# Two-layer gated cross-attention with experts: where layer 1's attention takes its statistics and moments

## The reference, cut to what matters

```python
x = x + jnp.tanh(g_xattn[0]) * _L0_xattn_ref(_layernorm(x), ctx, ctx, ...)   # 16 heads
x = x + jnp.tanh(g_ffn[0])   * _L0_ffn_ref(_layernorm(x), ...)               # 8 experts, each token takes its best 2
x = x + jnp.tanh(g_xattn[1]) * _L1_xattn_ref(_layernorm(x), ctx, ctx, ...)   # one head, causal mask
x = x + jnp.tanh(g_ffn[1])   * _L1_ffn_ref(_layernorm(x), ...)               # each expert takes its best 17 tokens of a sequence
```

## Time and profile before

| | us |
|---|---|
| median of 3 runs | 1018.54 |
| lowest and highest of them | 1015.94, 1024.3 |
| the profiled execution's own time | 1020.45 |
| its span, first to last instruction | 1018.6 |
| mean granted clock of TensorE, of full speed | 0.963 |

### The profile page before, as it was taken

One profiled execution on the slowest core, in us unless ns is written; L12 is line 12 of the kernel. 1 busy time (PEld: TensorE's weight loads), 2 busy tenths in 40 slices (PEclk: granted clock), 3 DMA queues, 4 the chain that ended last, 5 costly groups with the idle time before them and its releaser, 6 DMA issues.

```text
span 1018.6 us, 25355 instructions
## 1 busy us (share of the span) xinstructions
PE 901.6 (89%) x9084; PEld 745.5 (73%) x9084; DVE 590.7 (58%) x1580; ACT 550.4 (54%) x1313; POOL 645.3 (63%) x807
## 2 busy tenths in 40 slices
PE   5998999888439999999999989778998999999992
PEld 3776767667328989899999966655776766778881
DVE  5887989999526473245625669774635325433320
ACT  1787877776314545444654766535554555454440
POOL 6453455368753777677427777721886658878885
PEclk9999999999759999999999999898999999999996
DMA  9365333012524656776556663140444634565454
GB/s 369 120 198 170 140 143 129 27 60 72 180 84 138 215 166 209 216 214 191 167 183 194 189 241 105 58 125 31 100 42 48 134 27 53 99 88 55 51 57 44
DMA packets 130156, 130.73 MB, mean 128 GB/s; under 512 B 33010, under 2 KB 102770, under 8 KB 129138
## 3 DMA queue, kind: packets, MB, share of 16 engines
q1 hardware_dynamic: 99810, 91.66, 28.9%
q0 software_dynamic: 28928, 29.91, 17.8%
q10 hardware_dynamic: 1296, 7.54, 1.8%
HBM read 53.84 MB, written 49.62 MB: 102 GB/s over the span
## 4 chain that ended last, share of the span: by engine, by line
PE 60%; DVE 11%; issue 9%; POOL 8%; DMA 7%; ACT 4%; SPq 1%; ACTq 0%; POOLq 0%; DVEq 0%
PE psum L881 11%; PE psum L897 11%; PE psum L1070 8%; PE psum L1060 8%; PE psum L687 3%; PE psum L1024 3%; PE psum L674 2%; DVE w_sb L1211 2%; POOL xg L2072 2%; PE psum L704 2%; POOL work L2086 2%; PE psum L871 2%; POOL odd L2164 1%; DMA odd<-ln_sb,dest 1%; DMA x_sb<-in_x 1%
## 5 line engine op out<-in xcount | busy, mean ns | idle before, releaser
L1858 ACT ACTIVATE hid_sb<-psum,work 128x128 f32<-128x128 f32 (+1 forms) x424 | 145.4, 411 | 157.4 <-PE psum L881 155.4
L2086 POOL DMA_INDIRECT work<-yg,place x128 | 122.8, 959 | 62.6 <-issue 35.1
L881 PE MATMUL psum<-work 128*128 128x128 f32 (+1 forms) x848 | 151.7, 322 | 4.0 <-issue 3.7
L897 PE MATMUL psum<-w_sb,hid_sb 128*128 x1192 | 150.2, 275 | 0.0
L897 PEld LDWEIGHTS psum<-w_sb,hid_sb 128*128 128x128 f32 x1192 | 144.7, 192 | 2.1
L1060 PE MATMUL psum<-work,w_sb 128*128 128x272 f32 (+2 forms) x512 | 131.1, 397 | 5.1 <-ACT ctx_sb L1959 3.1
L881 PEld LDWEIGHTS psum<-work 128*128 128x128 f32 x848 | 125.1, 193 | 13.7 <-issue 6.3
L2164 POOL DMA_INDIRECT out_x<-ln_sb,dest x68 | 106.0, 1559 | 44.9 <-DVE ln_sb L1665 25.0
L2072 POOL DMA_INDIRECT xg<-work,place x104 | 100.5, 966 | 53.4 <-issue 25.6
L1959 ACT ACTIVATE ctx_sb<-psum,w_sb 128x272 f32<-128x272 f32 (+2 forms) x256 | 115.8, 487 | 26.4 <-PE psum L1060 22.6
L1070 PE MATMUL psum<-ctx_sb,w_sb 128*128 128x272 f32 (+2 forms) x512 | 128.1, 392 | 0.0
(11 more groups left out here) (264 smaller groups left out, 1570.0 us busy)
## 6 DMA issues: line engine op xcount, KB each, us to landing
work<-w_sb SPq DMA_DIRECT2D x76, 322.0 KB
work<-xg SPq DMA_DIRECT2D x73, 128.0 KB
yg<-yg_sb SPq DMA_DIRECT2D x73, 128.0 KB
xg<-yg_sb SPq DMA_DIRECT2D x24, 384.0 KB, 4.1
ctx_sb<-tok SPq DMA_DIRECT2D x8, 1088.0 KB, 6.2
ctxn<-sums_sb SPq DMA_DIRECT2D x64, 64.0 KB
out_x<-x_sb SPq DMA_DIRECT2D x16, 256.0 KB, 2.2
odd<-yg_sb SPq DMA_DIRECT2D x10, 384.0 KB, 3.1
```

Of the source, the lines that this page charges most:

```text
L881: e.matmul(banks[UP_BANKS[c]][:, 0:cols], w1g(b)[:, c * P:c * P + P], xgT_sb[:, u % 2, at:at + cols], start=True, stop=True).then_inc(s_up, 1)
L897: ins = e.matmul(banks[DOWN_BANKS[b % 2]][:, n * D:n * D + D], hid0[:, b % 2, c, n * P:n * P + P], w2_sb[:, bass.ds(number, 1), c, :].rear ...
L1858: e.activation(hid0[:, b % 2, c, 0:cols], banks[UP_BANKS[c]][:, 0:cols], ACT.Gelu, bias=w1g(b)[:, HID + c:HID + c + 1]).then_inc(s_hg, 1)
L2086: e.indirect_dma_start(dst[:, k, :], None, yg_dram[h], at).then_inc(s_get[i], 16)
```

## The change

Routing starts two steps earlier, in step 5. The lists leave behind the store of group 9 instead of 11. Six tiles are picked in the loop instead of four, in steps 13 to 15. From step 3 on `LATER_BY` is one tile behind the old one, from step 5 on two. Router statistics of groups 0 to 3 are taken in steps 2 to 5 and those of groups 4 to 7 in steps 12 to 15. GpSimd's order becomes: gathers 48 and 49, `moments1(40)`, gathers 50 to 55, one chain of router moments for all 16 tiles, gathers 56 to 59, `moments1(48)`, gathers 60 to 63, `moments1(56)`, one chain for tiles 16 to 31. A chain over n tiles counts its semaphore by n // 8, so that the waits on it stay as they are.

```diff
--- before.py
+++ after.py
@@ -103,7 +103,7 @@
 
 NORM1_FROM = NBLK[0] + NBLK[1] + 14
 
-ROUTE1_FROM = 7
+ROUTE1_FROM = 5
 
 
 ROUTE_IN = {NP - 1: 1, NP: 2, NP + 1: 1, NP + 2: 1}
@@ -111,10 +111,10 @@
 COUNT_AT, SOFTMAX_AT, GATES_AT = 11, 12, 18
 
 
-SPREAD_AT = 11
-PICKED = {14: (0, 1), 15: (2, 3)}
-
-LATER_BY = (0, 1, 3, 5, 7, 9, 11, 13, 15, 16)
+SPREAD_AT = 9
+PICKED = {13: (0, 1), 14: (2, 3), 15: (4, 5)}
+
+LATER_BY = (0, 1, 3, 4, 6, 7, 9, 11, 13, 15, 16)
 
 
 def later_by(u):
@@ -123,6 +123,7 @@
 
 
 EARLY_ROUTER = 2 * NS // TG
+ROUTER_STATS = {2: 0, 3: 1, 4: 2, 5: 3, 12: 4, 13: 5, 14: 6, 15: 7}
 
 RING = 32
 
@@ -1628,8 +1629,8 @@
                     combine(t)
                     if t % TG == TG - 1:
                         statistics1(t // TG)
-                if 5 <= u < 5 + EARLY_ROUTER:
-                    statistics_router1(u - 5)
+                if u in ROUTER_STATS:
+                    statistics_router1(ROUTER_STATS[u])
                 if u >= ROUTE1_FROM:
                     next(side, None)
                 for t in PICKED.get(u, ()):
@@ -2002,8 +2003,8 @@
                 if raised:
                     step.done(ins)
                     ins = e.tensor_scalar(nmr[:, lo:lo + n], nmr[:, lo:lo + n], 1.0, None, ALU.add)
-                ins.then_inc(s_done, 1)
-                made[s_done.num] += 1
+                ins.then_inc(s_done, n // TS or 1)
+                made[s_done.num] += n // TS or 1
                 w.wait_ge(s_done, made[s_done.num])
 
             def moments_twice(router, first):
@@ -2118,8 +2119,8 @@
             def moments1(lo):
                 moments(lo, TS, s_st2, lo + TS, s_mom1, raised=True)
 
-            def moments_router1(lo):
-                moments(lo, TS, s_st3, lo + TS, s_mom2)
+            def moments_router1(lo, n=TS):
+                moments(lo, n, s_st3, lo + n, s_mom2)
 
 
             for t in range(PARTS[-1][0]):
@@ -2134,12 +2135,12 @@
                 get(t)
                 if t == PARTS[-1][0] + 1:
                     moments1(PARTS[-1][0] - TS)
-            moments1(PARTS[-1][0])
-            for lo in range(0, NS, TS):
-                moments_router1(lo)
+                if t == PARTS[-1][0] + 7:
+                    moments_router1(0, NS)
+                if t == PARTS[-1][0] + 11:
+                    moments1(PARTS[-1][0])
             moments1(NT - TS)
-            for lo in range(NS, 2 * NS, TS):
-                moments_router1(lo)
+            moments_router1(NS, NS)
```

## The result

| | before | after |
|---|---|---|
| median, us | 1018.66 (4 runs) | 1027.26 (4 runs) |
| lowest and highest | 1015.94, 1024.3 | 1025.33, 1029.66 |
| ratio, 95% interval | | 1.0083 (1.0049 to 1.0117) |
| profiled execution, its span | 1020.45, 1018.6 | 1025.33, 1023.5 |
| attention stage | 99.5 | 109.0 |

The ratio is worth 5 to 12 us, with 8.5 in the middle. The forecast was 1022, inside a range of 1013 to 1029.

A forecast was written before the change was run, and what follows sets the result against it. It took attention's path through GpSimd's late gathers and moments, VectorE's routing, the lists and TensorE's gathers as the bound. The first expert product moves from 695.2 to 698.9 us, +3.7 on the median 1018.54, giving 1022; range 1013 to 1029.

The forecast's parts named there:

- costs twice: Rival: ScalarE's stop keeps TensorE at the lower clock through groups 12 to 15 and the gathers; +7 us, 1029; chance 0.14.
- Steps (1) and (2): VectorE's router statistic 3 ends at 629.4 us; GpSimd's merged chain waits 6.7 us for it, then takes 5.4.
- Step (3): GpSimd's gathers resume 0.4 us after a chain, one each 1.24, landing 2.5 after start; tile 56 at 639.1, 60 at 653.5.
- Step (4): VectorE waits for gathers 5.6 us in group 6, 0.7 in 7, 2.6 in 8; last statistics end at 668.6.
- Step (5): Moments of tiles 56 to 63 at 673.0 us stop ScalarE in group 11; TensorE's slow clock then costs 1.6 us.
- Step (6): Lists issued behind group 9 are there at about 675 us, before group 13's picks; VectorE's 1.86 us wait goes.
- Step (7): Groups 12 to 15 and last gathers: group 15 opens at 690.8, experts at 698.9; the tail gains 4.4 us.
- Step (8): Router statistics 4 to 7 in groups 12 to 15 with one chain cost zero; without cover, a chain of 5.4 us.
- one-to-one shift: Assumption that a shift of the experts' first product moves the kernel's end by the same amount.
- GpSimd's wait not binding: Rival: the statistic is there when tile 55's gathers end; experts start at about 692.6, -2.6 us, 1016; chance 0.17.
- All idle time won: Rival: VectorE's idle 5.24 and 1.86 us and the tail's 4.4 won, no new wait; -11 us, 1007; chance 0.06.
- nothing moves: Rival: the old and new waits cancel, time 1018.5 us; chance 0.13.

The follow-up runs named there:

- e6b: e6 measured again on another chip: ratio to the kernel before 0.9972, attention stage 94.1 us.
- e5: Changed kernel with the lists issued behind group 11 and four tiles picked in the loop, as before: ratio 1.0043 to the kernel before, on the disturbed chip.
- e8: Changed kernel with router statistics 4 to 7 in groups 6 to 9 instead of 12 to 15: ratio 1.0064 to the kernel before, on the disturbed chip.
- e2: Changed kernel with the router chain for tiles 0 to 15 behind the gathers of tile 59 instead of 55: ratio 1.0028 to the kernel before.
- e4: Changed kernel with routing from group 7, lists behind group 11 and four picks, as in the kernel before: ratio 1.0087 to the kernel before.
- e1: Changed kernel with the router chain for tiles 0 to 15 behind the gathers of tile 57 instead of 55: ratio 1.0074 to the kernel before.
- e7b: e7 measured again: ratio to the kernel before 1.0043, attention stage 102.0 us.
- e9: e6b with router statistics 4 to 7 in groups 6, 7, 10 and 11 instead of 12 to 15: ratio 0.9940 to the kernel before.
- e6: e2 with the last tile combined in group 9 instead of 10: ratio 1.0003 to the kernel before, on the disturbed chip.
- e7: Changed kernel with old combines, routing from group 6, lists behind 10, router chain behind tile 59, moments 48 to 55 behind 61: ratio 0.9994, disturbed chip.

## Why the prediction was right in its direction and too small

The chain of causes was the forecast one, and the sum was 5.8 us of the stage too small. The time lies inside the range, but its upper end was set mainly by the rival "costs twice", which isn't what happened; that the range held is in part luck. The forecast of 3.7 us itself is outside the measured interval of 5 to 12.

**Steps (1) and (2)** held to 0.2 us. From the stage's start to the end of router statistic 3 I had 33.7 us, measured 33.6. GpSimd's wait: 6.7 forecast, 6.68 measured. The chain: 5.4 forecast, 5.6 measured.

**Step (3) failed in size.** It had gathers resume 0.4 us after a chain, one each 1.24 us, and land 2.5 us after their start. Tile 56 landed 11.8 us after the statistic instead of 9.7, tile 60 27.8 instead of 24.1. Of these 3.7 us 2.0 are the gap between the two gathers of tile 56. The largest of the others is tile 60's flight, 3.7 us from its second start (648.72 to 652.38), where I had one row with 2.5; the rest is in the chains, a few tenths longer than forecast, and in the first gather after a chain, 1.39 us from start to start. The bound that the prediction gave for the pace, "0.1 x 16 more", covers less than half of the 3.7 (the gap of 0.4 that it calls ScalarE's is GpSimd's in the earlier trace rows).

**Step (4)** is the right mechanism: waits in groups 6, 7 and 8 of 7.2, 1.4 and 2.5 us, forecast 5.6, 0.7 and 2.6. Last statistics 43.5 us after router statistic 3, forecast 39.2: step (3)'s 3.7 and 0.6 more, of which 0.44 is a wait for TensorE in group 10 that I had put at nothing.

**Step (5)** held: last statistics to group 11's output product 6.3 us, forecast 6.3; ScalarE's stop 4.0; the slow projections are there, 1.92 against 1.02. But it priced a wait without asking what sets it. e6b answers: the last combine's group, 5.9 us of the stage.

**Step (6)** held in that no wait for the lists is left. **Step (7) failed by 1.6 us**: 25.6 from group 11's product to the experts, forecast 24.0. All of it lies in the last group. Group 15 opens on VectorE 15.9 us after group 11's product, as forecast (the step's own terms add up to 0.4 more than its 690.8), and from there to the experts it is 9.7 us instead of 8.1. The term was the gathers, counted at full clock: four of the six behind group 15's product ran slow, and VectorE waits 1.75 and 0.25 us for gathers before its last picks of the loop, which the step doesn't have. In e6b, with the product and all six at full clock, the same end is 1.4 us shorter, so the clock is nearly all of the 1.6. The "tail gains 4.4" was 2.8: 12.5 us before, 9.7 after. In the kernel before all eight gathers ran at 1.0 us each. What paid for the gain is seen in e5 and e8: a pair of picks costs the groups before as much as it saves behind them, and the statistics cost 1.0.

**Step (8)** puts the chain for tiles 16 to 31 at nothing. It runs from 693.28 us on, beside the last gathers, and nothing in the stage waits for it.

The sum: 3.7 forecast, plus 4.3 from (3) and (4), plus 1.6 from (7), less 0.1, is the 9.5 us of the stage. The one-to-one shift held in this pair of traces (323.4 and 323.5 us behind it); in other traces the part behind is up to 2 us longer, whatever the kernel.

**The rivals.** "GpSimd's wait not binding" wasn't what happened, and e2, where GpSimd has no such wait either, speaks against its price: the stage was 0.5 us longer than before, where I gave it 2.6 less. The last combine's wait in step (5) stays without the first one. "Costs twice", 1029, was nearer to the measured 1027.3 than the forecast and had 0.14; but its mechanism, the lower clock from 675 on, isn't in the trace: groups 12 to 14 ran at full clock from 679 on, and only the product of group 15 and four gathers were slow again. "All idle time won" and "nothing moves" are out.

## What to carry to other kernels

A chain with an input from another engine, put in front of a queue of transfers, delays everything queued behind it by its wait and its own length; before moving one, write down when its input is ready and put it at the first place after that. Merging two short dependent chains was a gain by itself (a wait 2.4 us shorter here), and it should be tried at the old place first. When parts of a kernel vary from execution to execution, compare the stage that the edit touches, from its own first to its last instruction, and not the spans; and look at what follows it in the same traces before setting a stage against a time.

## What the runs showed of the hardware that I had not expected

GpSimd paused 2.00 us between two indirect transfers that wait for nothing, at the same instruction in all four kernels with the chain behind tile 55 (after and e4, and e5 and e8 on the other chip), and no gap of that length stands there in any kernel with the chain elsewhere.

TensorE's clock at the end of the stage went with the version, and what in the version decides it isn't shown. Behind the same rests of 1.57 and 0.90 us in group 15, the way from that group's product to the experts took 7.3 to 7.5 us in after, e1, e2 and e7b, 6.1 in e6b and 8.4 in e9, all with six gathers there. The two kernels that were traced twice gave the same both times (e6 and e6b 6.1; e7 7.5 and e7b 7.4). The slow products some 85 us into the experts are another matter: there the same kernel shows 2.33 us in one trace and 4.0 in the other (e6 and e6b, e7 and e7b). Together the two can move a comparison of two traces by up to 4 us.

And one chip ran the kernel before in 1253 us where others took 1018 to 1020. The traces of the versions on it show waits that they put to no instruction on VectorE and ScalarE, up to some 40 us long (in e6), all ahead of the last 350 us of the execution. From the first expert product on, these traces take 323.4 to 323.6 us, as the kernel before does elsewhere.
